# A unit of quantised cross attention moved between two of self attention, and the experts' ends spread over more steps

## The chip, the cores and the metric

The kernel runs on one core of a Trainium2 chip. The metric is the device time of one execution in microseconds; lower is better. Five engines work side by side, each with its own instruction stream: TensorE (PE), VectorE (DVE), ScalarE (ACT), GpSimd (POOL) and SyncE (SP, which here only issues transfers). They are ordered among each other by semaphores alone.

## The reference, cut to what matters

Four sequences of 512 tokens (width 128, 16 heads of 8) go through four layers. The part that the change touches is the third layer's two attentions and the tail of the second layer's mixture of experts:

```python
# layer 2, the end: two of eight experts a token
h = gelu(x @ w1[e] + b1[e]); eo = h @ w2[e] + b2[e]
x = layernorm(x + sum_over_two_experts(combine * eo))
# layer 3: eight-bit rounding of q, k, v and of the probabilities
def attn(x, ctx):
    q, k, v = x @ wq, ctx @ wk, ctx @ wv
    sim  = fq(q) @ fq(k).T * 8 ** -0.5
    out  = fq(softmax(sim)) @ fq(v)
    return out @ wo + bo
x = attn(ln1(x), ln1(x)) + x          # 512 keys a head
x = attn(ln2(x), context) + x         # 154 keys a head
x = x + ff(ln3(x))
```

The sequences don't depend on each other. Within a sequence the context attention needs the result of the self attention before it.

## The kernel before

Work is counted in units: unit `u` is stage `u // 4` of sequence `u % 4`. Units 16 to 19 are the quantised self attentions of the four sequences, 20 to 23 their context attentions, and 12 to 15 the experts of the four sequences. All quantised units run through one software pipeline of steps, listed in `QUANT_STEPS`: 32 steps for a self unit, 16 for a context unit, 192 in all. Before, the units come in the order 16, 17, ..., 23.

One step handles two heads of one tile of 128 queries against 512 keys (self), or four against 154 (context):

- PE makes the scores into one of three banks (L1258), and in every second step weighs the values with the codes of two earlier steps (L1277).
- DVE first inverts the sums of the step two before (L2037, L2038), takes the row maxima of this step's scores (L2044), and turns the half-precision codes of the step six before into the form that PE reads (L2027).
- ACT scales the maxima (L1553) and takes the exponentials with their sums (L1562).
- POOL scales the inverted sums (L2257, self only) and rounds the probabilities to codes (L2268). ACT may be at most three steps ahead of POOL.
- SP issues one transposing transfer a step (L904).

`schedule()` hangs other work on the steps: `at(quant, slot, (name, unit))` puts an item behind the step's own work, on each engine that has a part in it. So an item on DVE delays that engine's part of the next step. The items in question:

- `Q`, `K`, `V`: a projection on PE and then the rounding on DVE for the next unit. `K` writes four masked copies, 512 wide for a self unit and 154 for a context unit.
- the copy of the weighed values into `oT` by DVE (L2052), always nine steps into the next unit (`QUANT_LAST`), and then `W`: the output projection on PE (L1014), the residual sum on DVE (L1739), the statistics (L1633, L1636, L1643), and a power on POOL (L2134).
- `M`: the normalisation on DVE (L1659), and a sum on POOL (L2138). `H`: transposes on PE (L941) and a copy on ACT (L1453), from which the next stage's `Q` reads.
- `g`: one gather of 128 expert rows by an indirect transfer from POOL's queue (L2215). Each sequence has eight.
- `M4a`: DVE waits for the eight gathers, makes eight scaled sums (L1764), and takes the statistics; POOL takes the power. `M4b`: normalisation on DVE, then two sums on POOL (L2192, L2138). `M5a`: DVE waits for those (`x_ready`) and takes the second statistics, POOL the power. `M5b`: normalisation on DVE, one sum on POOL. `H` as above.

Before, the gathers of unit 14 hang on steps 5, 8, ..., 26 of unit 16, and its `M4a`, `M4b`, `M5a`, `M5b`, `H` on steps 0, 2, 4, 6, 8 of unit 17. The gathers of unit 15 hang on steps 5, 8, ..., 26 of unit 17, and its ends on steps 0, 2, 4, 6, 8 of unit 18.

Of the kernel before, what the change touches and what calls it, by code (L numbers as in the profile page):

```python
# [7 lines left out]
P = 128  # L8
HEADS, HD = 16, 8
TILES = TOKENS // P  # L10
# [4 lines left out]
ROUND = 1.5 * 2.0 ** 23  # L15
# [8 lines left out]
QUANT_LAG, WEIGH_LAG, GROUPED_LAG = 6, 8, 2  # L24
# [36 lines left out]

STAGES = 9
L0, SELF, CROSS, MOE, QSELF, QCROSS, FF0, GQA, FF1 = range(STAGES)
EXACT_UNITS, QUANT_UNITS = range(0, 12), range(16, 24)


def stage(u):
# [7 lines left out]
def is_cross(u):  # L75
    return stage(u) in (L0, CROSS, QCROSS)
# [94 lines left out]

QUANT_BASE, QUANT_STEPS = {}, []
for u in QUANT_UNITS:
    QUANT_BASE[u] = len(QUANT_STEPS)
    QUANT_STEPS += [(u, n) for n in range(16 if is_cross(u) else 32)]
QUANT_BASE[QUANT_UNITS[-1] + 1] = len(QUANT_STEPS)

QUANT_LAST = {QUANT_BASE[u + 1] + WEIGH_LAG + 1: u for u in QUANT_UNITS}  # L180


def quant_step(n):
# [16 lines left out]
def at(table, slot, *items):  # L200
    table.setdefault(slot, []).extend(items)


def schedule():
# [52 lines left out]
    for u, first in ((12, 16), (13, 15), (14, 15)):  # L257
        f = FIRST_SLOT[u - 3] + first
# [18 lines left out]
              (half + 20, "V", 16), (half + 21, "H", 13)]  # L277
    for slot, *item in items:
        at(moe, slot, tuple(item))
    for u in QUANT_UNITS:  # L280
        f, per = QUANT_BASE[u], QUANT_BASE[u + 1] - QUANT_BASE[u]
        if u == 16:

            for v in (14, 15):
                first = QUANT_BASE[v + 2]
                for n in range(2 * TILES):
                    at(quant, first + 5 + 3 * n, ("g", v, n))
                for slot, name in ((0, "M4a"), (2, "M4b"), (4, "M5a"), (6, "M5b"), (8, "H")):
                    at(quant, QUANT_BASE[v + 3] + slot, (name, v))
        else:  # L290
            for slot, name in zip((10, 12, 14) if per == 16 else (10, 12, 13), "WMH"):
                at(quant, f + slot, (name, u - 1))
        if u + 1 in QUANT_UNITS:
            for slot, name in zip((8, 9, 11) if per == 16 else (15, 18, 22), "QKV"):
                at(quant, f + slot, (name, u + 1))
    for slot, *items in ((0, ("W", 23), ("zg", 24)), (1, ("gK", 28, 0)), (2, ("M", 23)), (3, ("gK", 28, 1)), (4, ("H", 23)),
                         (5, ("gK", 28, 2)), (6, ("D", 24)), (7, ("gK", 28, 3)), (8, ("M", 24)), (9, ("H", 24), ("gV", 28)),
                         (10, ("D", 25), ("gqa", 28, 0)), (11, ("gqa", 28, 1)), (12, ("M", 25)), (13, ("H", 25), ("gqc", 28, 0)),
# [97 lines left out]
def build(nc, io, out):  # L396
# [3 lines left out]
    with ctx:  # L400
# [382 lines left out]
        with nc.Block() as block:  # L783
# [145 lines left out]
            def _(pe):  # L929
# [17 lines left out]
                def item(name, u, n=None):  # L947
# [60 lines left out]
                    elif name == "W":  # L1008
                        if u < 12:
                            pe.wait_ge(misc_read, out_of("N2", u))  # L1010
                        else:
                            pe.wait_ge(oT_ready, u - 15)
                        for t in range(TILES):
                            ins = nc.tensor.matmul(misc_t[:, t, :], oT[:, t * P:(t + 1) * P], w_of(u, 3),  # L1014
                                                   start=True, stop=True)
# [231 lines left out]
                def scores_quant(i):  # L1247
                    u, t, a, h, heads = quant_step(i)
                    n = CTX if is_cross(u) else TOKENS
                    if i == QUANT_BASE[u]:  # L1250
                        pe.wait_ge(q_coded, u - 15)
                        pe.wait_ge(k_coded, u - 15)
                    if i >= 3:
                        pe.wait_ge(quant_exp, i - 2)
                    for z in range(heads):
                        for j in range(2):
                            r = 32 * (2 * a + j)
                            ins = nc.tensor.matmul(quant_score[i % 3][:, j, z * n:(z + 1) * n],  # L1258
                                                   qT_codes[r:r + 32, u % 2, t * P:(t + 1) * P],
                                                   k4_codes[r:r + 32, u % 2, h + z, 0:n], start=True, stop=True)  # L1260
                    ins.then_inc(quant_scored, 1)

                def weigh_pair(n):

                    u, t, _, first, heads = quant_step(2 * n)
                    pe.wait_ge(codes_copied, 2 * n + 2)
                    if 2 * n == QUANT_BASE[u]:
                        pe.wait_ge(v_coded, u - 15)
                        if u > 16:
                            pe.wait_ge(oT_ready, u - 16)  # L1270
                    tiles = 2 if is_cross(u) else TILES
                    for z in range(heads):
                        i = first + z
                        for k in range(tiles):
                            vals = v_quant_tail[:, u % 2, :, :] if is_cross(u) and k else v_quant[:, u % 2, k, :, :]
                            for j in range(4):
                                ins = nc.tensor.matmul(acc[32 * j:32 * j + 32, P * t:P * (t + 1)], vals[:, 4 * j + i, :],  # L1277
                                                       pT_codes[:, (2 * n + j // 2) % CODE_SLOTS, j % 2 * TILES + tiles * z + k, :],
                                                       start=(i == 0 and k == 0), stop=(i == 3 and k == tiles - 1))
                    ins.then_inc(pair_weighed, 1)  # L1280
# [342 lines left out]
            def _(dve):  # L1623
# [63 lines left out]
                def item(name, u, n=None):  # L1687
# [189 lines left out]
                    elif name == "Q" and u in QUANT_UNITS:  # L1877
# [2 lines left out]
                                                ALU.mult, ALU.add).then_inc(misc_read, 1)  # L1880
                        dve.wait_ge(misc_read, m + 1)
                        then(nc.vector.tensor_scalar(q_round, q_round, ROUND - 128.0, ROUND + 127.0, ALU.max, ALU.min))
                        nc.vector.tensor_scalar(qT_codes[:, u % 2, :], q_round, -ROUND, None, ALU.add).then_inc(q_coded, 1)
                    elif name == "K" and u in QUANT_UNITS:
                        width = CTX if is_cross(u) else TOKENS
                        dve.wait_ge(misc_raised, m + 1)
# [3 lines left out]
                        then(nc.vector.tensor_scalar(k_round[:, 0:width], k_round[:, 0:width], ROUND - 128.0, ROUND + 127.0,  # L1890
                                                     ALU.max, ALU.min))
                        for j in range(4):
                            ins = nc.vector.tensor_scalar(k4_codes[:, u % 2, j, 0:width], k_round[:, 0:width], -ROUND,
                                                          head_mask[:, j:j + 1], ALU.add, ALU.mult)
                        ins.then_inc(k_coded, 1)
                    elif name == "V" and u in QUANT_UNITS:
# [8 lines left out]
                        for k, rows_k in tiles:  # L1905
                            then(nc.vector.tensor_scalar(v_round[0:rows_k, k, :], v_round[0:rows_k, k, :], ROUND - 128.0,
                                                         ROUND + 127.0, ALU.max, ALU.min))
                            for i in range(4):
                                if is_cross(u):
                                    to = v_quant_tail[0:rows_k, u % 2, :, :] if k else v_quant[:, u % 2, 0, :, :]  # L1910
                                    to = to.rearrange("p (j i) c -> p j i c", i=4)
                                    of = v_round[0:rows_k, k, :].rearrange("p (j i d) -> p j i d", i=4, d=HD)
                                else:
                                    to = v_quant[:, u % 2, :, :, :].rearrange("p t (j i) c -> p (t j) i c", i=4)
                                    of = v_round.rearrange("p t (j i d) -> p (t j) i d", i=4, d=HD)
                                ins = nc.vector.tensor_scalar(to[:, :, i, HD * i:HD * (i + 1)], of[:, :, i, :], -ROUND, None,
                                                              ALU.add)
# [114 lines left out]
                for i in range(quant_steps + WEIGH_LAG + 2):  # L2032
                    if 2 <= i < quant_steps + 2:
                        t, v_ = of_step(total, i - 2), of_step(inv_total, i - 2)
                        dve.wait_ge(quant_exp, i - 1)
                        if is_cross(QUANT_STEPS[i - 2][0]):
                            then(nc.vector.tensor_scalar(t, t, sizes[:, 7:8], None, ALU.mult))  # L2037
                        nc.vector.reciprocal(v_, t).then_inc(quant_inv, 1)  # L2038
                    if i < quant_steps:
                        src = quant_score[i % 3][:, :, :]  # L2040
                        if is_cross(QUANT_STEPS[i][0]):
                            src = src[:, :, 0:2 * CTX].rearrange("p j (z k) -> p j z k", z=2)
                        dve.wait_ge(quant_scored, i + 1)
                        nc.vector.tensor_reduce(of_step(top_score, i), src, axis=AX.X, op=ALU.max,  # L2044
                                                negate=True).then_inc(quant_top, 1)
                    if QUANT_LAG <= i < quant_steps + QUANT_LAG:
                        copy_codes(i - QUANT_LAG)
                    if i in QUANT_LAST:
                        u = QUANT_LAST[i]
                        dve.wait_ge(pair_weighed, QUANT_BASE[u + 1] // 2)  # L2050
                        of = stage(u) - QSELF
                        nc.vector.tensor_scalar(oT[:, :], acc[:, :], out_scale[:, of:of + 1], None, ALU.mult)\  # L2052
                            .then_inc(oT_ready, 1)
                    for it in QUANT_ITEMS.get(i, ()):
                        item(*it)
# [310 lines left out]
```

## Time and profile before

| | |
|---|---|
| median of 3 runs | 1616.45 us (1616.28 to 1617.36) |
| the profiled execution | 1629.24 us, span 1627.4 us |
| busy over the span | PE 1109.7, DVE 1109.3, ACT 895.0, POOL 681.6 us |
| the 192 quantised steps | 737.3 to 1209 us of the span, 471.7 us |
| self units 16, 17, 18, 19 | 74.5, 86.7, 81.3, 71.7 us |
| context units 20, 21, 22, 23 | 39.9, 40.2, 40.3, about 37 us to the last step's start |

The units are marked off by their first row maximum on DVE (L2044 occurs 192 times, once a step, in the order of `QUANT_STEPS`). Busy times add up per engine and overlap between engines. An engine's idle time has a cost only where the engine is the one that the others wait for.

### The profile page before, as it was taken

To read this page: it belongs to the slowest core of one execution; us is meant where nothing else is said; L and a number is where in the kernel's file an instruction comes from. 1 tells how busy PE (TensorE), PEld (TensorE's weight loads), DVE (VectorE), ACT (ScalarE), POOL (GpSimd) and SP (SyncE) were. 2 spreads that over 40 slices of the span, in tenths; PEclk is the share of its full clock that TensorE was granted. 3 is DMA by queue.
4 is the path that set the end of the run, shared out by engine and by line. 5 is a ranking of instruction groups with operands and counts; after the bars stand their busy time and mean duration, and the time that the engine had idled before them with its cause. 6 is when DMAs were issued, how large, how long until landed. Compare 5 with 4: busy or idle time off the path is not lost.

```text
span 1627.4 us, 28786 instructions
## 1 busy us (share of the span) xinstructions
PE 1109.7 (68%) x9344; PEld 600.2 (37%) x9344; DVE 1109.3 (68%) x3126; ACT 895.0 (55%) x2546; POOL 681.6 (42%) x1054
## 2 busy tenths in 40 slices
PE   2688888787777679784435354444439787898888
PEld 1333344444322238681111121122215544453545
DVE  2577777777666666277989899877765556666533
ACT  1344455545543346347767688888872344545542
POOL 3321010111011323456888888877771245354420
PEclk9899999999998999796555555555559889999999
DMA  6223242022172111217546566655650112111000
GB/s 175 62 47 72 49 120 92 10 72 48 32 150 42 35 41 52 74 40 182 116 95 111 97 110 118 120 109 107 106 106 1 26 40 53 33 28 46 3 1 26
DMA packets 263829, 115.86 MB, mean 71 GB/s; under 512 B 216056, under 2 KB 252544, under 8 KB 261504
## 3 DMA queue, kind: packets, MB, share of 16 engines
q1 hardware_dynamic: 258720, 107.61, 31.6%
q0 software_dynamic: 2048, 4.20, 0.9%
q10 hardware_dynamic: 2912, 2.22, 0.5%
q8 instruction: 75, 1.23, 0.3%
q14 instruction: 74, 0.61, 0.1%
HBM read 38.80 MB, written 16.45 MB: 34 GB/s over the span
## 4 chain that ended last, share of the span: by engine, by line
PE 35%; POOL 19%; issue 17%; DVE 15%; ACT 10%; DMA 2%; SPq 1%; POOLq 0%; another core or an unknown queue 0%; ACTq 0%; DVEq 0%
POOL arena L2268 10%; ACT arena L1562 5%; PE acc L1177 3%; PE trans L1149 2%; POOL inv_total L2257 2%; PE misc L999 2%; PE misc L1005 2%; PE trans L1301 2%; ACT arena L1509 2%; POOL arena L2215 2%; PE score L1313 2%; PE score L1315 2%; PE trans L1155 2%; PE acc L1175 1%; DVE arena L1727 1%
## 5 line engine op out<-in xcount | busy, mean ns | idle before, releaser
L2268 POOL TENSOR_SCALAR arena<-arena,inv_total 128x512 f16<-128x512 f32 (+1 forms) x512 | 302.6, 591 | 55.8 <-DVE inv_total L2038 15.4
L1960 DVE TENSOR_REDUCE minus_top<-score 128x4 f32<-128x616 f32 (+4 forms) x256 | 201.4, 803 | 140.9 <-PE score L1110 54.6
L2134 POOL TENSOR_TENSOR rstd<-spread,minus_half 128x4 f32<-128x4 f32 x36 | 37.7, 1048 | 526.1 <-DVE spread L1643 456.9
L1562 ACT ACTIVATE arena<-score,minus_top,exp_scale 128x512 f32<-128x512 f32 (+1 forms) x340 | 210.6, 626 | 18.1 <-POOL arena L2268 8.1
L1509 ACT ACTIVATE arena<-trans 128x512 f32<-128x512 f32 x240 | 134.5, 596 | 113.8 <-PE trans L1155 107.8
L1600 ACT ACTIVATE arena<-arena,minus_top 128x154 f32<-128x154 f32 x256 | 105.1, 412 | 133.0 <-DVE minus_top L2103 132.9
L1258 PE MATMUL score<-arena 32*128 32x512 bf16 (+1 forms) x340 | 69.0, 458 | 144.1 <-ACT arena L1562 143.2
L2044 DVE TENSOR_REDUCE top_score<-score 128x2 f32<-128x1024 f32 (+1 forms) x128 | 135.7, 1061 | 0.6 <-PE score L1258 0.5
L2288 POOL TENSOR_TENSOR arena<-arena,inv_total 128x512 f32<-128x512 f32 x64 | 66.7, 1041 | 147.4 <-DVE inv_total L2111 133.6
L1562 ACT ACTIVATE arena<-trans,minus_top,exp_scale 128x154 f32<-128x154 f32 (+1 forms) x172 | 105.6, 621 | 16.2 <-POOL arena L2268 11.8
L2098 DVE CUSTOM_DVE_ANT_0 arena<-score,arena 128x154 f32<-128x154 f32 x256 | 66.0, 314 | 62.8 <-PE score L1338 62.4
L2027 DVE TENSOR_SCALAR arena<-arena 128x1024 bf16<-128x1024 f16 x192 | 102.7, 535 | 5.5 <-DMA arena<-arena 5.5
L1553 ACT ACTIVATE minus_top<-top_score,exp_scale 128x2 f32<-128x2 f32 (+1 forms) x192 | 56.5, 294 | 61.4 <-DVE top_score L2044 61.1
L1258 PEld LDWEIGHTS score<-arena 32*128 32x128 bf16 x340 | 14.3, 102 | 195.4 <-ACT arena L1562 178.0
L1177 PE MATMUL acc<-arena 128*32 128x512 f32 (+3 forms) x768 | 80.6, 507 | 4.7 <-issue 4.0
L1258 PE MATMUL trans<-arena 32*128 32x154 bf16 (+1 forms) x172 | 34.7, 451 | 72.0 <-ACT arena L1562 71.8
L1106 PE MATMUL score<-arena 64*128 64x154 bf16 x512 | 45.7, 248 | 54.0 <-issue 32.7
L1527 ACT ACTIVATE arena<-score,arena 128x128 f32<-128x128 f32 x184 | 52.0, 372 | 50.4 <-PE score L1214 43.4
L1277 PE MATMUL acc<-arena 128*32 128x128 bf16 x1536 | 59.2, 307 | 27.8 <-DVE oT L2052 15.2
L1509 ACT ACTIVATE arena<-trans,arena 128x512 f32<-128x512 f32 x80 | 52.3, 687 | 30.6 <-PE trans L1155 27.0
L2044 DVE TENSOR_REDUCE top_score<-trans 128x2 f32<-128x1024 f32 (+1 forms) x64 | 67.4, 1053 | 0.0
L1447 ACT COPY arena<-misc 128x512 bf16<-128x512 bf16 x48 | 28.1, 586 | 70.1 <-PE misc L989 67.3
(282 smaller groups left out, 2902.6 us busy)
## 6 DMA issues: line engine op xcount, KB each, us to landing
arena<-q_terms SPq DMA_DIRECT2D x176, 64.0 KB
late<-arena SPq DMA_DIRECT2D x128, 64.0 KB, 2.0
q_terms<-arena SPq DMA_DIRECT2D x36, 128.0 KB
late<-k_terms SPq DMA_DIRECT2D x64, 64.0 KB
arena<-arena SPq DMA_TRANSPOSE x192, 3.1
by_expert<-zeros SPq DMA_DIRECT2D x2, 1472.0 KB, 17.6
arena<-by_expert SPq DMA_DIRECT2D x10, 256.0 KB, 3.0
from_expert<-arena SPq DMA_DIRECT2D x10, 256.0 KB
```

The source lines that it names most:

```text
L1177: ins = nc.tensor.matmul(acc[32 * j:32 * j + 32, q0:TOKENS], v_cols[:, k, 4 * g + j, :], src, start=(b % half == 0 and k == 0), stop=(last ...
L1258: ins = nc.tensor.matmul(quant_score[i % 3][:, j, z * n:(z + 1) * n], qT_codes[r:r + 32, u % 2, t * P:(t + 1) * P], k4_codes[r:r + 32, u % ...
L1277: ins = nc.tensor.matmul(acc[32 * j:32 * j + 32, P * t:P * (t + 1)], vals[:, 4 * j + i, :], pT_codes[:, (2 * n + j // 2) % CODE_SLOTS, j % ...
L1509: nc.scalar.activation(expT[w % SLOTS], trans[w % 2][:, :], ACT.Exp, bias=bias)\
L1562: ins = nc.scalar.activation(probs[:, i % 3, j, of], quant_score[i % 3][:, j, of], ACT.Exp, bias=minus_top[:, at_col:at_col + 1], scale=ex ...
L1600: ins = nc.scalar.activation(gq_exp_p[:, i % 3, h, :], shifted[:, i % 3, h, :], ACT.Exp, bias=minus_top[:, at_col:at_col + 1], accum_out=t ...
L1960: nc.vector.tensor_reduce(dst, src, axis=AX.X, op=ALU.max, negate=True).then_inc(top_ready, 1)
L2027: nc.vector.tensor_scalar(pT_codes[:, of, :, :].rearrange("p k q -> p (k q)"), pT_raised[:, of, :, :].rearrange("p k q -> p (k q)"), -HALF ...
L2044: nc.vector.tensor_reduce(of_step(top_score, i), src, axis=AX.X, op=ALU.max, negate=True).then_inc(quant_top, 1)
L2098: ins = nc.vector.tensor_tensor_reduce(out=shifted[:, i % 3, h, :], in0=score[i % 2][:, odd, z * CTX:(z + 1) * CTX], in1=mask_add[:, b % 2 ...
L2268: ins = nc.gpsimd.tensor_scalar(codes[:, (i - 1) % CODE_SOURCES, j, to], probs[:, (i - 1) % 3, j, of], inv_total[:, at_col:at_col + 1], HA ...
L2288: nc.gpsimd.tensor_tensor(gq_p[:, v % 2, :, :], gq_exp_p[:, v % 3, :, 0:P], inv.to_broadcast([P, 4, P]), ALU.mult)
```

## The change

The context unit of sequence 0 goes between the self units of sequences 1 and 2: `QUANT_UNITS` becomes 16, 17, 20, 18, 19, 21, 22, 23. Everything that used `u - 15` or `u % 2` uses the unit's place in that list (`QUANT_PLACE`). The items' slots change with it:

| item | before | after |
|---|---|---|
| `W`, `M`, `H` in a self unit | 10, 12, 13 | 10, 13, 15 |
| `W`, `M`, `H` in a context unit | 10, 12, 14 | 9, 12, 14 |
| `Q`, `K`, `V` in a self unit | 15, 18, 22 | 17, 20, 24 |
| `Q`, `K`, `V` in a context unit | 8, 9, 11 | 8, 6, 11 |
| gathers of 15 | 17: 5, 8, ..., 26 | 17: 5, 12, 19, 26; 20: 1, 5, 9, 13 |
| `M4a`, `M4b`, `M5a`, `M5b`, `H` of 14 | 17: 0, 2, 4, 6, 8 | 17: 19, 23, 27, 30; 20: 1 |
| the same of 15 | 18: 0, 2, 4, 6, 8 | 20: 15; 18: 2, 5, 8, 10 |

The number of instructions is the same on every engine.

```diff
-EXACT_UNITS, QUANT_UNITS = range(0, 12), range(16, 24)
+EXACT_UNITS = range(0, 12)
+
+QUANT_UNITS = [16, 17, 20, 18, 19, 21, 22, 23]
+QUANT_PLACE = {u: n for n, u in enumerate(QUANT_UNITS)}
...
+    for k, u in enumerate(QUANT_UNITS):
+        f, per = QUANT_BASE[u], QUANT_END[u] - QUANT_BASE[u]
+        if k:
+            for slot, name in zip((9, 12, 14) if per == 16 else (10, 13, 15), "WMH"):
+                at(quant, f + slot, (name, QUANT_UNITS[k - 1]))
+        if k + 1 < len(QUANT_UNITS):
+            for slot, name in zip((8, 6, 11) if per == 16 else (17, 20, 24), "QKV"):
+                at(quant, f + slot, (name, QUANT_UNITS[k + 1]))
+
+    for n in range(2 * TILES):
+        at(quant, QUANT_BASE[16] + 5 + 3 * n, ("g", 14, n))
+        at(quant, QUANT_BASE[17] + 5 + 7 * n if n < 4 else QUANT_BASE[20] + 4 * (n - 4) + 1, ("g", 15, n))
+    for v, name, u, slot in ((14, "M4a", 17, 19), (14, "M4b", 17, 23), (14, "M5a", 17, 27), (14, "M5b", 17, 30), (14, "H", 20, 1),
+                             (15, "M4a", 20, 15), (15, "M4b", 18, 2), (15, "M5a", 18, 5), (15, "M5b", 18, 8), (15, "H", 18, 10)):
+        at(quant, QUANT_BASE[u] + slot, (name, v))
...
-                            pe.wait_ge(oT_ready, u - 15)
+                            pe.wait_ge(oT_ready, QUANT_PLACE[u] + 1)
```

## Rows read from the trace of the kernel before

**Rows 1.** Windows, unit 18: length, busy us of PE, PEld, DVE, ACT, POOL.
```profile
898.50:979.80 81.30, 37.13 (x350) 14.83 (x350) 75.40 (x162) 60.46 (x163) 66.98 (x105) 0.52 0.58 106
```

**Rows 2.** Waits of ACT in units 17, 18, 19: us, times, longest.
```profile
ACT minus_top L1553 <- DVE top_score L2044: 16.4, 9, 3.8
ACT arena L1562 <- POOL arena L2268: 8.1, 13, 1.4
...
ACT minus_top L1553 <- DVE top_score L2044: 17.3, 9, 3.8
ACT arena L1562 <- POOL arena L2268: 0.8, 3, 0.4
...
ACT minus_top L1553 <- DVE top_score L2044: 8.9, 6, 3.0
```

**Rows 3.** Waits of ACT in units 20, 21 and 23.
```profile
ACT minus_top L1553 <- DVE top_score L2044: 3.6, 4, 1.3
...
ACT minus_top L1553 <- DVE top_score L2044: 3.3, 3, 1.1
...
ACT minus_top L1553 <- DVE top_score L2044: 1.8, 2, 1.6
```

**Rows 4.** Timeline of unit 17, `M4a` to `M5a`, then `W`: start, us, [idle before].
```profile
819.44 0.30 ACT L1553 ACTIVATE minus_top<-top_score,exp_scale 128x2 f32<-128x2 f32 x1 [3.78 <-DVE top_score L2044]
821.45 1.50 DVE L1659 TENSOR_SCALAR normed<-y,moments,rstd 128x128 f32<-128x128 f32 x4 [0.19 <-POOL rstd L2134]
824.18 0.30 ACT L1553 ACTIVATE minus_top<-top_score,exp_scale 128x2 f32<-128x2 f32 x1 [0.81 <-DVE top_score L2044]
828.21 0.87 DVE L1633 BATCH_NORM_STATS2 stats<-x 128x6 f32<-128x128 f32 x4 [1.15 <-POOL x L2138]
831.37 0.30 ACT L1553 ACTIVATE minus_top<-top_score,exp_scale 128x2 f32<-128x2 f32 x1 [3.24 <-DVE top_score L2044]
841.67 2.08 PE L1014 MATMUL misc<-attn_w,oT 128*128 128x128 f32 x8
843.78 0.69 DVE L1739 TENSOR_TENSOR x<-misc,x 128x512 f32<-128x512 f32 x1 [1.28 <-PE misc L1014]
```

**Rows 5.** Timeline of a context unit in steps without items, DVE and ACT.
```profile
1060.40 0.77 DVE L2044 TENSOR_REDUCE top_score<-score 128x4 f32<-128x616 f32 x1
1062.12 0.30 ACT L1553 ACTIVATE minus_top<-top_score,exp_scale 128x4 f32<-128x4 f32 x1
1062.27 0.23 DVE L2037 TENSOR_SCALAR total<-total,sizes 128x4 f32<-128x4 f32 x1 [0.77 <-ACT arena L1562]
```

**Rows 6.** Timeline, DVE: `K` self in unit 18; maxima of steps 8, 14, `oT` in 22.
```profile
949.39 1.20 DVE L2044 TENSOR_REDUCE top_score<-score 128x2 f32<-128x1024 f32 x1
954.04 1.20 DVE L2044 TENSOR_REDUCE top_score<-trans 128x2 f32<-128x1024 f32 x1
...
1150.15 0.77 DVE L2044 TENSOR_REDUCE top_score<-score 128x4 f32<-128x616 f32 x1
1154.21 0.74 DVE L2052 TENSOR_SCALAR oT<-acc,out_scale 128x512 f32<-128x512 f32 x1
1167.56 0.77 DVE L2044 TENSOR_REDUCE top_score<-score 128x4 f32<-128x616 f32 x1
```

**Rows 7.** A gather in unit 17, and the landing of the unit's eight.
```profile
869.41 1.00 POOL L2215 DMA_INDIRECT arena<-from_expert,row_no  x1 [0.27 <-issue]
...
DMA to landing us min/median/max: 3.3/3.4/3.6
```

**Rows 8.** Timeline of unit 20, its last steps on POOL and DVE.
```profile
1085.71 2.07 POOL L2268 TENSOR_SCALAR arena<-arena,inv_total 128x154 f16<-128x154 f32 x4 [0.33 <-DVE inv_total L2038]
1087.86 1.34 POOL L2138 TENSOR_TENSOR x<-x,rows 128x512 f32<-128x512 f32 x1
1090.04 0.42 DVE L2027 TENSOR_SCALAR arena<-arena 128x1024 bf16<-128x1024 f16 x1
```

**Rows 9.** Waits of DVE, 680 to 720 us: `M4a` of the first sequence.
```profile
DVE y L1764 <- DMA arena<-from_expert,row_no: 2.5, 1, 2.5
```

## The prediction on record

> **What bounds the kernel now.** I read the page for the span, then the windows of the eight units, then the waits of ACT and DVE in each unit, then the timeline around the items. The profiled execution took 1629.24 us with a span of 1627.4, against a median of 1616.45 for the runs; I work out a difference from that execution and add it to the median. Less than 0.2% (3.2 us) is what a measurement of this kernel can't tell from no change.
>
> In the quantised stretch no engine is full: in unit 18 ACT is busy 60.5 of 81.3 us, DVE 75.4, POOL 67.0 [rows 1]. Yet ACT sets the pace: in steps without items DVE waits for its exponentials, and ACT finds its maxima ready [rows 5]. So a unit lasts 32 or 16 such steps plus what ACT stands idle, and that idle time has two owners. It waits for DVE's row maxima when an item holds DVE up: 16.4 us in unit 17, 17.3 in 18, 8.9 in 19. It waits for POOL's codes, because only three steps of probabilities have a place: 8.1 us in unit 17, which has eight gathers, 0.8 in unit 18, which has the same items without them [rows 2]. In context units it waits 3.6 and 3.3 us for DVE, 1.8 in the last, which prepares nothing [rows 3]. The change touches these two idle times and no instruction's duration, so I cost it in ACT's waiting alone.
>
> **Unit 17, POOL.** A gather holds POOL for 1.0 us, with 0.27 idle before it [rows 7]: 1.3 each, 10.4 for eight. Against unit 18 they cost ACT 7.3 us (8.1 less 0.8). Four of them leave. The other four stand seven steps apart and mostly near an item at which ACT stands still anyway and POOL catches up. Bounds: 0.8 (all hidden) and 8.1 (nothing gained). I take 0.8 plus 4 x 0.6 = 3.3, nearer the low end because POOL's load falls by 5.2 us. That is -4.8.
>
> **Unit 17, DVE.** The unit keeps a whole end of an expert sequence (now that of 14 on steps 19 to 30) and prepares a context unit in place of a self unit. The single waits of ACT behind `M4a`, `M4b`, `M5a` are 3.78, 0.81, 3.24 us [rows 4]. In the second, DVE itself had waited 0.19 for the power, in the third 1.15 for POOL's two sums [rows 4]. With three or four steps between them instead of two, these waits go: 3.8 + 0.6 + 2.1, and 0.6 for `M5b`. Unit 19 holds `W`, `M` and the preparation of a context unit for 8.9 in all [rows 2], less 0.2 as `M` moves to three steps behind `W`. Sum 3.8 + 0.6 + 2.1 + 0.6 + 8.7 = 15.8 for 16.4: -0.6.
>
> **Unit 18.** `M4a` leaves (-3.8), the same waits go (-1.15 - 0.2 - 0.2 - 0.2): 17.3 becomes 11.8, -5.5. POOL keeps most of its extra work in a unit that is 5 us shorter, so I let its 0.8 become 1.8 (bounds 0.8 and 4): +1.0. **Unit 19** loses 0.2. **Unit 16** keeps its gathers and its items' durations; moving `Q`, `K`, `V` by two steps in a unit filled by POOL I cost at nothing; if POOL weren't the cover there, their three waits could move by a few tenths.
>
> **Context units: the ledger.** In a quiet context step DVE idles 0.77 us, and its maxima are ready 0.95 us before ACT needs them (1061.17 against 1062.12) [rows 5]. So an item of D us makes DVE late by D - 0.8; what exceeds 0.95 is ACT's wait, and 0.95 of lateness stays, of which each free step takes back 0.8. Item durations come from the starts of the maxima. The seven of steps 8 to 14 in unit 22 begin at 1150.15, 1153.18, 1156.75, 1160.25, 1163.62, 1166.11 and 1167.56 (the first and the last are shown) [rows 6]. The last gap, 1.45, is DVE's free step (with the 0.77 idle the pace is 2.22); the others less 1.45 are `Q` 1.6, `oT` with `K` 2.1, `W` 2.1, `V` 1.9, `M` 1.0. I round them up by 0.1, except `W`, for the start of an item that the free step hides. `oT` alone is 0.74 [rows 6], so `K` context is 1.5. `K` self is the gap of 4.65 less a free self step of about 1.6: 3.05 [rows 6]. `M4a` is ACT's wait of 3.78 and the 0.95 of lead together, 4.7 [rows 4]. I test it on unit 21 as it is: `Q` on step 8, `oT` with `K` (2.2) on 9, `W` on 10, `V`, `M` on 12 give 0 + 1.35 + 1.3 + 1.2 + 0.3 = 4.15; the trace has 3.3 [rows 3]. So I multiply by 0.8.
>
> After the change `K` comes alone on step 6 and costs nothing, but `W` stands on step 9, directly behind `oT`. PE needs 2.08 us for `W` and can't begin before `oT`; in self units, with a step of DVE's work in between, DVE still waits 1.28 us [rows 4]; here it has nothing in between and waits 2.2. That item is 0.74 + 2.2 + 2.1 = 5.0. Behind it are PE's next scores, which DVE needs later than PE is free, so no second wait. Ledger: 0 + 0 + 4.15 + 0.4 + 0.3 = 4.85, times 0.8 is 3.9, against 3.3: +0.6 for each of **units 21 and 22**. In **unit 23**, where no `K` was in the way before, 1.8 becomes 2.9: +1.1. The low end for each is nothing, if the wait falls in DVE's idle time, the high end the whole 2.2.
>
> **Unit 20** now prepares a self unit: `K` 3.05 on step 6 costs 1.3, `Q` 0.1, the step 9 item 4.2, `V` 0.5, `M` 0.3. On step 15 comes `M4a`, 4.7 - 0.8 - 0.95 = 2.95 of it seen by ACT. Sum 9.35, times 0.8 is 7.5. And `M4a` waits for the last gather, which hangs on step 13. The same place in the unit as it is now [rows 8]: POOL does the sum of `M` on step 12 until 1089.2, then step 12's codes (2.07 us) until 1091.4; a gather could start at 1091.7 and land 3.4 later [rows 7], at 1095.1. DVE is through with step 15's own work at 1090.46. So DVE waits about 4.5 us in full, and ACT with it: 7.5 + 4.5 = 12.0 for 3.6, +8.4 (bounds for the 4.5: nothing, if POOL has caught up, and 5). That gathers are waited for where they stand close is seen once already, 2.5 us [rows 9]. POOL comes into the unit late from `M5b` on step 30, has only some 0.15 us to spare in a step (2.22 less 2.07 [rows 8]), and gets gathers on steps 1 and 5 ahead of any item: +1.5 (bounds 0 and 4).
>
> The page of the Trainium skill "DMA: Bandwidth & Descriptors", section "Anatomy of one DMA — SWDGE (gpsimd) path", fits about 2.0 us plus bytes over 436 GB/s for such a transfer, 2.15 us for 64 KB by estimate. The gathers here took 3.4, so the row decides; by the page's figure the wait would be 1.2 us shorter and the sum 0.9 instead of 2.1.
>
> **The sum.** Unit 17 -5.4, 18 -4.5, 19 -0.2, 20 +9.9, 21 and 22 +1.2, 23 +1.1: +2.1 us. On the profiled execution that is 1631.3, on the median 1618.5, within what can't be told from no change. In words: what is won in units 17 and 18 is paid in unit 20.
>
> **The rivals.**
> - *The late rows are in time and the gathers hide.* If POOL runs a step less behind in the fuller unit 20 (DVE's long stop on step 9 lets it catch up), the wait before `M4a` shrinks to about 1, -3.5; and if the four gathers in unit 17 hide wholly, another -2.3. 2.1 - 5.8 = -3.7: 1612.8. For it: POOL idles in those stops. Against: rows 8 already stand behind such a stop.
> - *Slower: POOL's backlog at the head of unit 20.* `M5b`'s sum and two gathers, 1.3 + 2 x 1.3 = 3.9 us, meet a POOL with nothing to spare until `K` on step 6; ACT sees all of it rather than 1.5, and the lag passes on to `M4a` by another 1. 2.1 + 2.4 + 1 = +5.5: 1622.0. It decides from 1.1 us above my figure on. Against: three steps of buffer in between.
> - *The spreading doesn't relieve POOL in unit 17.* Unit 17 now has all its POOL work in its last two thirds, while its first nine steps run straight behind the POOL-filled unit 16 without the stop that `M4a` gave. If its wait stays at 8.1 instead of 3.3: +6.9, 1623.3.
>
> **Chances.** My forecast 0.38, in time 0.28, backlog 0.20, no relief 0.14. So faster 0.28, the same 0.38, slower 0.34. The range goes from a little below the first rival's time to a little above the last's, 1611 to 1625; the forecast's own, with the small bounds alone, is 1616 to 1620.
>
> **What would show it.** Right: windows of unit 17 and of unit 18 each some 5 us shorter; unit 20 near 50 us; a wait of DVE's L1764 for the gathers of 3 to 5 us; DVE's L1739 waiting 2 us for PE in each context unit; the 1.15 before L1633 gone. Wrong: no wait at L1764, or ACT waiting over 4 us for L2268 in unit 20, or over 6 in unit 17.

## The result, and the profile after

The changed kernel is slower: 1629.83 us (median of 20 runs) against 1617.36 us (20 runs of the kernel before), a ratio of 1.0073 with a 95% interval of 1.0048 to 1.0098. On the 1616.45 of the prediction that is some 1628, above the range's top of 1625. The same file in a second set of runs gave 1.0039 (1.0011 to 1.0067), some 1623 on the same median and inside that range, so the size of the loss is less sure than its sign: 6 to 12 us.

The spans don't show it: 1625.9 us in this profile against 1627.4 before. What the change touches can be read by itself, though: the 192 quantised steps, from the first row maximum to the last. They begin at 727.1 us of the span now and at 737.3 before, though nothing ahead of them was edited, and they last 479.1 us now against 471.7.

The windows of the changed kernel for its first four units, 16, 17, 20 and 18 in the order in which they now run (columns as in [rows 1]):

```profile
727.00:802.10 75.10, 30.82 (x272) 10.09 (x266) 60.51 (x104) 57.97 (x157) 59.65 (x95) 0.52 0.71 155
802.10:883.30 81.20, 34.42 (x344) 13.09 (x344) 75.36 (x167) 59.67 (x162) 68.81 (x107) 0.50 0.59 108
883.30:937.10 53.80, 22.08 (x238) 10.66 (x238) 38.16 (x111) 37.83 (x151) 38.86 (x73) 0.53 0.58 97
937.10:1013.50 76.40, 35.80 (x330) 14.31 (x330) 70.72 (x145) 58.56 (x158) 65.17 (x103) 0.50 0.56 104
```

Unit by unit, by the starts of the row maxima in both traces: 17 and 18 are 5.5 and 4.9 us shorter, 19 by 0.4, 16 is 0.6 longer, 20 is 14.0 longer (53.8 for 39.8), and 21, 22, 23 are 0.9, 1.3 and 1.5 longer. Sum +7.4.

Unit 20's long step, as the timeline of the changed kernel shows it:

```profile
927.06 0.59 DVE L2029 TENSOR_SCALAR arena<-arena 128x1024 bf16<-128x1024 f16 x1
929.62 1.01 POOL L2217 DMA_INDIRECT arena<-from_expert,row_no  x1 [0.27 <-issue]
933.05 2.05 DVE L1766 SCALAR_TENSOR_TENSOR y<-arena,weight,y 128x128 f32<-128x128 f32 x7 [5.40 <-DMA arena<-from_expert,row_no]
938.38 0.30 ACT L1555 ACTIVATE minus_top<-top_score,exp_scale 128x2 f32<-128x2 f32 x1 [7.04 <-DVE top_score L2046]
```

DVE is through with step 15's own work at 927.65. POOL issues the last gather two microseconds later and the rows land 3.4 after that, so `M4a` stands for 5.40 us, and ACT for 7.04. Step 9 of the same unit is the other place:

```profile
909.58 0.74 DVE L2054 TENSOR_SCALAR oT<-acc,out_scale 128x512 f32<-128x512 f32 x1
910.47 2.05 PE L1016 MATMUL misc<-attn_w,oT 128*128 128x128 f32 x8 [6.07 <-DVE oT L2054]
912.55 0.69 DVE L1741 TENSOR_TENSOR x<-misc,x 128x512 f32<-128x512 f32 x1 [2.23 <-PE misc L1016]
915.20 2.07 POOL L2270 TENSOR_SCALAR arena<-arena,inv_total 128x154 f16<-128x154 f32 x4 [4.32 <-DVE inv_total L2040]
915.83 0.30 ACT L1555 ACTIVATE minus_top<-top_score,exp_scale 128x4 f32<-128x4 f32 x1 [4.12 <-DVE top_score L2046]
```

DVE makes `oT`, PE starts on it at once, and DVE has nothing to do in the meantime; before, 1.28 us of such a wait stood in self units [rows 4] and none in unit 20. POOL doesn't catch up in this stop. Its next codes need the sums that DVE inverts, so it stands idle for 4.32 us as well, then has a power and a gather to do, and ACT waits another 0.86 us for it on step 12. Of the 3.3 us that ACT waits for POOL in this unit, 2.1 lie on steps 0 to 5 and 1.2 on steps 12 and 15.

ACT's waits in the changed kernel, units 17, 20, 18 (us in all, times, longest), to be set beside [rows 2, 3]:

```profile
ACT minus_top L1555 <- DVE top_score L2046: 13.4, 8, 4.3
ACT arena L1564 <- POOL arena L2270: 6.8, 18, 1.6
...
ACT minus_top L1555 <- DVE top_score L2046: 5.8, 3, 4.1
ACT arena L1564 <- POOL arena L2270: 3.3, 6, 1.2
...
ACT minus_top L1555 <- DVE top_score L2046: 14.1, 6, 7.0
ACT arena L1564 <- POOL arena L2270: 6.5, 9, 2.9
```

The 7.0 falls on the border of 20 and 18 and belongs to unit 20: 12.8 there, 7.1 in unit 18. Over all the steps ACT waits 60.6 us for DVE (61.1 before) and 28.7 us for POOL (19.6 before). Only 3.3 of the 9.1 that POOL's column grows by are in unit 20; 5.7 are in unit 18, which is shorter all the same. So the column in which a wait is booked doesn't say where the time was lost.

### The profile page after: what moved, and what is told of

It is laid out like the page before. It is cut to its first block, busy times and chain, and to the rows that moved or that the text cites. A ratio compares the mean times of both kernels' runs of the same rounds, so it can differ in the third digit from the quotient of the medians.

```text
span 1625.9 us, 28786 instructions
## 1 busy us (share of the span) xinstructions
PE 1104.5 (68%) x9344; PEld 595.4 (37%) x9344; DVE 1105.3 (68%) x3126; ACT 895.1 (55%) x2546; POOL 681.2 (42%) x1054
## 4 chain that ended last, share of the span: by engine, by line
PE 36%; DVE 21%; issue 14%; POOL 13%; ACT 12%; DMA 2%; SPq 1%; POOLq 0%; ACTq 0%; DVEq 0%
POOL arena L2270 7%; ACT arena L1564 6%; DVE top_score L2046 3%; PE acc L1179 3%; PE trans L1151 2%; PE misc L1001 2%; PE misc L1007 2%; PE trans L1303 2%; ACT arena L1511 2%; PE score L1315 2%; PE score L1317 2%; PE trans L1157 2%; PE acc L1177 2%; PE misc L1016 2%; DVE arena L2029 1%
## 5 line engine op out<-in xcount | busy, mean ns | idle before, releaser
L1564 ACT ACTIVATE arena<-trans,minus_top,exp_scale 128x512 f32<-128x512 f32 (+1 forms) x170 | 105.3, 626 | 19.1 <-POOL arena L2270 15.0
L1260 PE MATMUL trans<-arena 32*128 32x512 bf16 (+1 forms) x170 | 35.0, 459 | 82.3 <-ACT arena L1564 82.3
L1555 ACT ACTIVATE minus_top<-top_score,exp_scale 128x2 f32<-128x2 f32 (+1 forms) x192 | 56.5, 294 | 60.8 <-DVE top_score L2046 60.6
L1529 ACT ACTIVATE arena<-score,arena 128x128 f32<-128x128 f32 x184 | 52.4, 370 | 41.0 <-PE score L1216 40.9
L1564 ACT ACTIVATION_READ_ACCUMULATOR arena<-score,minus_top,exp_scale 128x1 f32 x342 | 67.0, 196 | 0.0
```

The costliest lines, as they stand in the source:

```text
L1564: ins = nc.scalar.activation(probs[:, i % 3, j, of], quant_score[i % 3][:, j, of], ACT.Exp, bias=minus_top[:, at_col:at_col + 1], scale=ex ...
```

## The experiments

Each was profiled and timed in 12 runs. An interval of such a ratio is about 0.6% wide, or 10 us, so the experiments are read by the length of the steps in the profile. That length repeats: 471.7 and 471.8 us in two profiles of the kernel before, 479.1 and 478.0 in two of the changed one, and 466.7 and 468.2 in two of the last version below. So a difference of under 1.5 us between two single profiles shows nothing. All differences below are of this length, and "the changed kernel" stands for its two profiles.

**The changed kernel again.**

> The changed kernel once more, to see what of its time comes back. In its first profile the 192 quantised steps took 479.1 us from the first maximum to the last against 471.7 before (+7.4), while the ratio of the timed runs says 0.73% (+11.8 us). Theory A (all of the loss lies in the quantised steps; the remainder is scatter of the runs): the steps take 479 within 1 us again, and the ratio is nearer to 1.005. Theory B (the change also slows what comes after the steps): the stretch from the last step to the end is some 4 us longer than before in this profile too, and the ratio stays at 1.007 or above.

The steps take 478.0 us, 1.1 less than in the first profile and just outside A's 1 us, and each unit is within 0.3 us of the first profile. The ratio is 1.0039 (1.0011 to 1.0067). From the last step's start to the end of the span are 412.8 us, against 419.8 in the first profile and 418.4 before. So the steps hold a loss of 6.2 to 7.4 us that comes back, and no loss behind them does: A.

**The last gathers earlier.**

```diff
-        at(quant, QUANT_BASE[17] + 5 + 7 * n if n < 4 else QUANT_BASE[20] + 4 * (n - 4) + 1, ("g", 15, n))
+        at(quant, QUANT_BASE[17] + 5 + 7 * n if n < 4 else QUANT_BASE[20] + 3 * (n - 4) + 1, ("g", 15, n))
```

> The last four gathers of unit 15 on steps 1, 4, 7, 10 of unit 20 instead of 1, 5, 9, 13; nothing else. Theory A (M4a on step 15 stands waiting for the gather of step 13, 5.4 us of the profile): the wait is gone, the quantised steps take about 474 us, 5 less than the changed kernel, and ACT's longest wait for the maxima falls from 7.0 to about 2. Theory B (POOL's load in unit 20 is what costs, and the wait only shows it): the wait turns into ACT's waits for POOL (3.3 us in the unit now, then 6 or more), and the steps stay at 477 to 479.

473.2 us, 4.7 to 5.9 less than the changed kernel, most of it in unit 20 (49.5 for 53.8 and 54.1). `M4a` waits for no gather any more, and ACT's wait on the border of the unit, behind `M4a`, is 1.8 us in place of 7.0. ACT's waits in unit 20, up to that border:

```profile
ACT minus_top L1555 <- DVE top_score L2046: 6.2, 3, 4.4
ACT arena L1564 <- POOL arena L2270: 3.8, 6, 1.2
```

The wait for POOL is 3.8 us where it was 3.3, not the 6 or more of B: A. Ratio 1.0032 (1.0006 to 1.0058).

**`W` on step 10.**

```diff
-            for slot, name in zip((9, 12, 14) if per == 16 else (10, 13, 15), "WMH"):
+            for slot, name in zip((10, 12, 14) if per == 16 else (10, 13, 15), "WMH"):
```

> The changed kernel with W on step 10 of the context units, as before, in place of step 9. Theory A (PE's 2.1 us for W stand bare behind oT on step 9): DVE's wait of 2.2 before the residual sum falls to 1.1 to 1.6 us in each of units 20 to 23, and the steps take some 2 us less, 477. Theory B (the cost in units 21 to 23, +0.9, +1.3 and +1.5 us, comes from K on step 6 and from M, which now have less room, not from W): no change, or a little slower, since V follows W at once.

471.2 us, 6.8 to 7.9 less. DVE's wait for PE falls from 2.2 us to 1.4 in units 20 to 22 and to 1.1 in 23, as A says, but the gain is more than three times what I expected of A: unit 20 takes 50.9 us, about 3 less; 21, 22 and 23 take 39.9, 40.4 and 37.0, less by 1.0 to 1.5 each. In unit 20 ACT's wait for POOL falls from 3.3 us to 1.8: what stood behind the stop on step 9 is gone, and POOL's own idle time there is 1.64 us for 4.32. The wait for the gathers is still there, 4.5 us. Ratio 1.002 (0.9987 to 1.0053).

**`W` on step 9 in the kernel before.**

```diff
-            for slot, name in zip((10, 12, 14) if per == 16 else (10, 12, 13), "WMH"):
+            for slot, name in zip((9, 12, 14) if per == 16 else (10, 12, 13), "WMH"):
```

> The kernel before with W on step 9 instead of 10 of the context units, and nothing else: the step of the prediction by itself. Theory A (bare behind oT, W makes DVE wait 2.2 us and costs that in part): DVE's wait for PE is 2.2 in each of four units, and the steps take 3 to 6 us more than 471.7. Theory B (the step costs only with K on 6 and V on 11 as in the changed kernel): under 2 us more.

481.2 us, +9.4 with one number changed, and a ratio of 1.0064 (1.0032 to 1.0096): A's mechanism, at half as much again as its upper bound of 6 us. Units 20, 21, 22 take 42.4, 43.0, 43.0 us, 2.6 to 2.7 more each, and 23 takes 1.5 more. The waits of unit 21 in this kernel:

```profile
ACT minus_top L1553 <- DVE top_score L2044: 6.2, 3, 5.5
DVE x L1739 <- PE misc L1014: 2.2, 1, 2.2
```

DVE's wait of 2.2 us is new in this unit, and ACT's rises by 2.9 over [rows 3], with a single wait of 5.5. Here `K` is on step 9 too, so `oT`, PE's 2.1 us, `W` and `K` follow one another. Moving `W` from 10 to 9 costs unit 21 2.7 us here, with `K` on 9 (40.3 to 43.0), and 1.0 to 1.3 in the new order with `K` on 6 (39.9 to 40.9 and 41.1). With `W` on 10, `K` on 6 gives nothing: 39.9 against 39.6 with `K` on 9 (the next experiment). So `K` on 6 pays only where `W` is on 9.

**The order alone.** The new order of units with every slot of before, the ends of 14 on steps 0 to 8 of unit 17, those of 15 on the same of 18, all gathers of 15 in unit 17.

```diff
-            for slot, name in zip((9, 12, 14) if per == 16 else (10, 13, 15), "WMH"):
+            for slot, name in zip((10, 12, 14) if per == 16 else (10, 12, 13), "WMH"):
...
-            for slot, name in zip((8, 6, 11) if per == 16 else (17, 20, 24), "QKV"):
+            for slot, name in zip((8, 9, 11) if per == 16 else (15, 18, 22), "QKV"):
...
```

> The new order of the units with all the slots of before: the ends of 14 on 0, 2, 4, 6, 8 of unit 17, those of 15 on the same of unit 18, all eight gathers of 15 in unit 17. Theory A (the order itself costs only what the larger K of a self unit costs in a context unit and saves in a self unit): the steps take within 2 us of the 471.7 of before. Theory B (the order is what costs, since POOL and DVE are worse matched after it): 476 us or more.

470.6 us: the order costs nothing that shows (it is 1.1 shorter, within what one file differs by from itself). Unit 20 takes 41.4 us, 1.6 more than before, with the self unit's `K` in it. So the 14.0 of unit 20 are 1.6 of the order and 12.4 of what was hung on it. Ratio 1.0005 (0.9976 to 1.0033).

**Both repairs together.** The last gathers on 1, 4, 7, 10 and `W` on 10.

> The changed kernel with both repairs: the last gathers on 1, 4, 7, 10 of unit 20, and W on step 10 of the context units. Alone they took the quantised steps from 478.5 (mean of two profiles of the changed kernel) to 473.2 and 471.2 us. Theory A (two separate stops of DVE, one ahead of M4a and one ahead of W's residual sum): the gains add, 466 us, 5.7 below the kernel before, and the time is about 0.3% below it. Theory B (both gains come from the same slack of POOL in unit 20): 469 to 471 us.

467.7 us, between A and B: 10.8 less than the mean of the changed kernel's two profiles, from which the two alone took 5.3 and 7.4. Unit 20 takes 47.1, which is still 7.3 more than before; this version is 4.0 below the kernel before because units 17 and 18 are 10.6 shorter. Ratio 0.9989 (0.9957 to 1.0022).

**`M4a` later.**

```diff
-                             (15, "M4a", 20, 15), (15, "M4b", 18, 2), (15, "M5a", 18, 5), (15, "M5b", 18, 8), (15, "H", 18, 10)):
+                             (15, "M4a", 18, 0), (15, "M4b", 18, 3), (15, "M5a", 18, 6), (15, "M5b", 18, 9), (15, "H", 18, 11)):
```

with `W` on 10 and the gathers as in the changed kernel.

> W on step 10, the gathers as in the changed kernel (last one on step 13 of unit 20), but M4a of 15 on step 0 of unit 18 and the rest on 3, 6, 9, 11. Theory A (M4a only has to stand later than the landing): no wait for the gathers or one below 1.5 us, but M4a now costs its 3.8 in a self step; the steps take about 468 us. Theory B (M4a is as good in one place as in the other and the 4.5 us wait of w_on_ten is what it costs): 466.5.

469.4 us, 1.8 less than with `W` on 10 alone, from which it differs only in these ends. `M4a` still waits 2.1 us for the gather of step 13, three steps ahead of it, where A allowed 1.5. Against both repairs together, unit 20 takes 43.2, 3.9 less with `M4a` out of it, and unit 18 takes 81.6, 5.4 more, of which 2.1 is the wait. That leaves 3.3 for `M4a` in a self step. The gathers stand elsewhere in the two runs, so 3.3 and 3.9 are no finer than some 0.5 us; but I had expected the self step to be the dearer one, and it isn't. Ratio 0.9991 (0.9961 to 1.0021).

**The spreading alone, in the old order.**

```diff
-                for slot, name in ((0, "M4a"), (2, "M4b"), (4, "M5a"), (6, "M5b"), (8, "H")):
+                for slot, name in ((0, "M4a"), (3, "M4b"), (6, "M5a"), (9, "M5b"), (11, "H")):
```

> The kernel before, in the old order, with the ends of 14 and 15 on steps 0, 3, 6, 9, 11 in place of 0, 2, 4, 6, 8 and nothing else. Theory A (as in the prediction: the waits of 1.15 us ahead of M5a and of 0.2 ahead of the normalisations go, twice): the steps take 2.5 to 3 us less than 471.7, and W on step 10 close behind costs nothing. Theory B (spreading gives nothing, since ACT waits for POOL in the same place): 471 to 472 us.

468.7 us, -3.0 as A says, but not where A says. Unit 18 is 1.9 us shorter, and 19 and 20 by 0.8 together; unit 17 isn't shorter at all (86.74 for 86.72). Its waits, then those of unit 18:

```profile
ACT arena L1562 <- POOL arena L2268: 12.7, 17, 1.7
ACT minus_top L1553 <- DVE top_score L2044: 12.3, 8, 3.8
...
ACT minus_top L1553 <- DVE top_score L2044: 12.7, 7, 3.8
ACT arena L1562 <- POOL arena L2268: 3.8, 6, 1.7
```

In unit 17, with eight gathers, the wait for DVE fell by 4.1 us against [rows 2] and the wait for POOL rose by 4.6. In unit 18 they are -4.6 and +3.0. The wait ahead of `M5a` is gone in both units. But in unit 17 DVE now waits 2.87 us for POOL's power ahead of `M` of step 12 (at 853.38), where the longest such wait was 0.9 before: POOL has a gather and the sum of `M5b`, now of step 9 instead of 6, to do shortly ahead of it. Ratio 0.9976 (0.9944 to 1.0008).

**The new order with the spreading, gathers all in unit 17.** Ends on 0, 3, 6, 9, 11 of units 17 and 18, `W`, `M`, `H` on 10, 13, 15 and `Q`, `K`, `V` on 17, 20, 24 of the self units, context slots as before.

> The new order with the ends on 0, 3, 6, 9, 11 of units 17 and 18, all gathers of 15 in unit 17 as before, W, M, H on 10, 13, 15 of the self units, Q, K, V on 17, 20, 24 there, and the old slots in the context units. The order alone took 470.6 us. Theory A: the spreading gives the same 2.5 to 3 us here, 468. Theory B (gathers and ends together fill POOL in unit 17, so the later Q, K, V cost more than the spreading gives): 470 or more.

469.7 us, 0.9 less than the order alone, which is within the scatter: nearer to B. Unit 17 takes 86.1 us against 86.4 with the order alone, as little helped as in the old order, though `M` is on 13 here and DVE's wait ahead of it is 0.9 us. ACT's wait for DVE in this unit is 6.5 us against 13.6 with the order alone, and its wait for POOL 18.8 against 11.1: what one gives up, the other takes. Ratio 0.9997 (0.9968 to 1.0026).

**A better version, twice.** Both repairs, `K` of the context units on 9 again, and four steps from `M4b` to `M5a` of 15:

```diff
-            for slot, name in zip((8, 6, 11) if per == 16 else (17, 20, 24), "QKV"):
+            for slot, name in zip((8, 9, 11) if per == 16 else (17, 20, 24), "QKV"):
...
-                             (15, "M4a", 20, 15), (15, "M4b", 18, 2), (15, "M5a", 18, 5), (15, "M5b", 18, 8), (15, "H", 18, 10)):
+                             (15, "M4a", 20, 15), (15, "M4b", 18, 2), (15, "M5a", 18, 6), (15, "M5b", 18, 9), (15, "H", 18, 11)):
```

> Both repairs, and besides K of the context units back on step 9 (unit 21 took 39.6 us with it there against 39.9 with it on 6), and M5a, M5b, H of 15 on 6, 9, 11 of unit 18, four steps behind M4b, for the wait of 1.2 us that M5a still has. Theory A: 467.7 less 0.3 for each of three context units and less 1.2 in unit 18 is 466; the time 0.3% below the kernel before. Theory B (K beside oT in unit 20 is the 3 us one of a self unit and takes back what it gives): 467.5.

> The same file as best once more, for the ratio and for how well its steps repeat. Theory A: the steps within 1 us of the first, the ratio within 0.3% of it, both below 1.

466.7 and 468.2 us, 5.0 and 3.5 less than before, and 1.5 apart where I had expected 1. The ratios are 0.9992 (0.9959 to 1.0026) and 0.994 (0.991 to 0.9969); they don't agree within the 0.3% that I had expected either. A's 466 and B's 467.5 can't be told apart by this, and neither can this version and the 467.7 of both repairs. The wait ahead of `M5a` is gone, but unit 18 takes 76.0 and 76.2 us, as with both repairs (76.2). In the timed runs one set shows the version faster than the kernel before and the other can't tell.

**The kernel before again.**

> The kernel before once more, for the scatter. Theory A (the quantised steps repeat, the rest scatters): the steps take 471.7 within 1 us, while their start and the stretch behind them move by several us; ratio 1.000. Theory B (the steps scatter too, so that differences of 5 us in them say little): more than 2 us off.

471.8 us, every unit within 0.1 us of the first profile. The steps begin at 726.5 instead of 737.3: A. Ratio 0.9993 (0.9961 to 1.0025).

## Why the prediction was wrong

The forecast was +2.1 us, "the same", with slower as the likeliest of the other two. The steps show +6.2 to +7.4, the timed runs +6 and +12. The two costs that it named are the ones that were there: mending both takes 10.8 us out of the steps, and the order by itself costs nothing. What failed is their size in unit 20.

- **Unit 17, -5.4, and unit 18, -4.5:** right in sum (-5.5, -4.9), though the parts were not. For unit 17 I had 15.8 us of waiting for DVE and 3.3 for POOL; it is 13.4 and 6.8. For unit 18 I had 11.8 and 1.8; it is 7.1 and 6.5. So that the sums came out is in part luck. The 6.8 is also over the 6 that I had given as a sign of being wrong. No run moves the four gathers alone, so how much of unit 17's gain is theirs isn't shown; with all eight in the unit, spreading the ends gave it 0.3 us or nothing. The wait of 1.2 us ahead of `M5a` went in unit 17, where four steps lie between, and stayed in unit 18, where there are three. Three can be enough (it went with three steps when the ends were spread in the old order), so the number of steps alone doesn't decide it.
- **Units 16 and 19,** nothing and -0.2: +0.6 and -0.4.
- **Units 21 to 23, +2.3:** 3.7. The ledger's stop on step 9 was sized rightly (DVE's wait 2.23 for 2.2), but two things were off: the 0.8 by which I multiplied came from a unit with short stops, and ACT saw 4.12 of a stop that it made 3.3; and I gave `K` a gain from step 6 that is there only to soften `W` on 9 (with `W` on 10, unit 21 takes 39.9 us with `K` on 6 and 39.6 with `K` on 9).
- **Unit 20, +9.9: this step failed.** It is +14.0. The mechanism, the last gather too late for `M4a`, was there to see; its term, 4.5, measured 5.4 in the first profile and 4.5 in the second, with ACT waiting 7.0 and 7.1 us behind it for the 6.9 that I had (2.95 times 0.8, and 4.5). ACT's waiting for DVE was 12.8 in all for my 12.0. The rest are POOL's term, 1.5, which measured 3.3, and a term that I left out. In POOL's term I saw only a late start into the unit. That part is 2.1; the other 1.2 comes later, on steps 12 and 15, behind the stop on step 9, and with `W` on 10 it is gone. The left-out term: `H` of unit 14 now runs on ACT inside this unit (L1455, on step 1), 0.8 us of work that no wait shows (unit 17 is rid of it, so it moves between units and adds nothing to the sum). Some 0.7 of the unit I can't place.
- **The rivals:** "no relief" (+6.9) came nearest in size, and not by its mechanism: unit 17 is 5.5 us shorter. Half of it holds, since ACT's wait for POOL fell there from 8.1 to 6.8 us only, not to 3.3. The backlog at the head of unit 20 (+5.5) is 2.1 us of ACT's wait for my 1.5, and most of the cost sits on steps 9 and 15, not at the head. The late rows weren't in time, and DVE's stop on step 9, which was to let POOL catch up, holds POOL up.
- **The landing:** the four gathers of unit 20 landed in 2.6 to 3.4 us, so the row was right to use. The estimate of 2.15 us that I had worked out from the Trainium skill ("DMA: Bandwidth & Descriptors", section "Anatomy of one DMA — SWDGE (gpsimd) path") is below all of them.

Over the whole, my terms say +4.4 us of waiting for DVE and -2.3 for POOL. The trace says -0.5 and +9.1. I costed the two owners one by one, as if the time taken from one were won. Spreading in place shows why that fails: in unit 17, 4.1 us taken from one came back as 4.6 in the other.

Of the first set's +11.8 us some 4 to 6 are in no part of a profile that repeats. The second set doesn't have them (+6.3). Whether they are scatter stays open, but the last section shows what such scatter goes with.

## What to carry to other kernels

In a software pipeline like this one, with three engines near balance, the length of a stretch isn't one sum of waits, because what one engine gives up another takes: take a wait from one engine only where the next one has room, and ask the windows first which units have it. An item that waits for another engine's answer to the instruction directly ahead of it belongs one step later; a single slot number cost 9.4 us here. A gather must be issued as many steps ahead as its queue lags, plus the landing; count both in time, from the same place of the trace, and read the effect in the edited stretch when whole runs scatter by more than it.

## What the runs showed of the hardware

The quantised steps repeat within 1.5 us from one profile to the next for the same file, but their start moved between 726.5 and 744.2 us over all the profiles, and what follows them took 412.0 to 424.6 us, with the same number of instructions on each engine every time. The two profiles of the changed kernel, from the last step's start to the end (columns as in [rows 1], with the granted clock third from the end):

```profile
1206.20:1625.90 419.70, 344.66 (x1980) 200.84 (x1980) 231.85 (x1004) 179.88 (x642) 144.85 (x187) 0.94 0.12 28
...
1209.20:1622.00 412.80, 336.32 (x1980) 197.65 (x1980) 232.13 (x1004) 179.94 (x642) 144.77 (x187) 0.96 0.12 28
```

The stretch goes with TensorE's granted clock: over the fourteen profiles the five shortest (412.0 to 416.4 us) had a mean of 0.95 or 0.96 in it and the five longest (422.2 to 424.6) had 0.93. PE is busy 336 us in the one and 345 in the other above, while DVE, ACT and POOL are within 0.3 us. Ahead of the steps the link is looser (0.95 for the start at 727, 0.93 for the one at 744). What moves the clock from one execution to the next isn't shown.

Inside the steps it is otherwise. The mean granted clock of a unit was 0.50 to 0.55 in every profile, at or near the lower of the two levels (1.2 GHz). Unit 23 of the kernel before had 0.55 in one profile and 0.50 in the other and took the same 37 us within 0.1. So the gains and losses of the steps are not ones of the clock.
